# Graph attention on one core: in the score stages VectorE sums six heads instead of four, and ScalarE builds the one-hot matrices

## The reference

```
q = (x @ Wq[l] + bq[l]).reshape(N, H, D)      # N 2500 nodes, H 8 heads, D 64
k = (x @ Wk[l] + bk[l]).reshape(N, H, D)
v = (x @ Wv[l] + bv[l]).reshape(N, H, D)
a = (q[dst] * k[src]).sum(-1) * scale         # one score for each edge and head
e = jnp.exp(a - amax[dst])
alpha = e / (denom[dst] + 1e-16)
agg = jax.ops.segment_sum(alpha[:, :, None] * v[src], dst, num_segments=N)
x = agg.reshape(N, C) + (x @ Ws[l] + bs[l]) + enc
```

## Time and profile before

| what | us |
|---|---|
| median of 3 runs | 2849.92 |
| the profiled execution | 2865.84 |
| its span, first to last instruction | 2864.0 |
| score stage of layer 0, first to last multiply | 114.3 to 709.6 |
| score stage of layer 1, first to last multiply | 1378.5 to 1972.3 |

### The profile page before, as it was taken

The page is one execution under the profiler, slowest core; times in us unless marked ns, Lnnn a source line. Parts: engine busy times, 40 slices in busy tenths (PEclk is TensorE's granted clock), DMA queues, the critical chain, the costliest instruction groups (busy, mean ns, idle before and its releaser), DMA issues. The chain is left out here.

```text
span 2864.0 us, 41493 instructions
## 1 busy us (share of the span) xinstructions
PE 2088.5 (73%) x7660; PEld 1573.9 (55%) x7661; DVE 1771.3 (62%) x2574; ACT 1526.7 (53%) x8378; POOL 1509.9 (53%) x1499
## 2 busy tenths in 40 slices
PE   8677778775366877778677777773566666677997
PEld 6455555553355656666455555542455555565786
DVE  7465666667655555556466666667554555567895
ACT  3266666666455455555466666664454554453221
POOL 1355555554665555551655555554555565544663
PEclk9888888887688888889798888886788888888999
DMA  8666767664666666653776767675555555543111
GB/s 300 224 205 206 220 199 221 210 205 149 202 178 187 192 191 190 191 181 117 238 212 211 216 201 215 203 214 159 159 154 154 156 167 155 156 123 129 52 67 43
DMA packets 201657, 511.74 MB, mean 179 GB/s; under 512 B 37916, under 2 KB 60572, under 8 KB 201191
## 3 DMA queue, kind: packets, MB, share of 16 engines
q0 software_dynamic: 112832, 369.71, 44.3%
q1 hardware_dynamic: 85862, 135.89, 14.2%
q10 hardware_dynamic: 2880, 5.24, 0.6%
HBM read 451.33 MB, written 59.06 MB: 178 GB/s over the span
## 5 line engine op out<-in xcount | busy, mean ns | idle before, releaser
L1255 PE MATMUL coll_banks<-coll_ev,coll_hot 128*128 128x260 f32 x2816 | 778.0, 435 | 301.0 <-DVE all_work L1359 257.9
L652 POOL DMA_INDIRECT all_work<-k_rows,all_work x704 | 673.7, 957 | 517.7 <-DVE all_work L881 280.0
L652 POOL DMA_INDIRECT coll_rows<-v_rows,coll_index x704 | 670.3, 952 | 502.6 <-issue 207.0
L1255 PEld LDWEIGHTS coll_banks<-coll_ev,coll_hot 128*128 128x128 f32 x2816 | 601.0, 218 | 457.4 <-DVE all_work L1359 258.3
L984 ACT ACTIVATE all_work<-all_work 128x64 f32<-128x64 f32 x2752 | 665.9, 243 | 233.0 <-issue 188.5
L846 PE MATMUL score_q_ps<-score_q,score_hot 128*128 x1408 | 474.2, 466 | 295.5 <-DVE score_hot L872 108.9
L881 DVE TENSOR_TENSOR all_work<-score_q_ps,all_work 128x1024 f32<-128x1024 f32 x352 | 430.2, 1222 | 381.5 <-remote 161.4
L984 ACT ACTIVATION_READ_ACCUMULATOR all_work<-all_work 128x1 f32 x2752 | 519.9, 189 | 160.3 <-issue 159.6
L1359 DVE TENSOR_TENSOR all_work<-all_work,coll_banks 128x520 f32 x352 | 244.3, 694 | 499.0 <-DMA score_w_raw<-in_Ws 177.2
L1515 ACT ACTIVATE coll_ev<-coll_rows,coll_e_now 128x64 f32<-128x64 f32 x2112 | 537.2, 333 | 0.0
L846 PEld LDWEIGHTS score_q_ps<-score_q,score_hot 128*128 128x128 f32 x1408 | 302.3, 225 | 422.8 <-issue 364.8
(11 more groups left out here) (251 smaller groups left out, 2342.2 us busy)
## 6 DMA issues: line engine op xcount, KB each, us to landing
score_xt<-x_turned SPq DMA_DIRECT2D x42, 512.0 KB
all_work<-k_rows,all_work POOLq DMA_INDIRECT x704
score_local<-local_dst SPq DMA_DIRECT2D x176, 64.0 KB
coll_rows<-v_rows,coll_index POOLq DMA_INDIRECT x704
x_turned<-keys_xt SPq DMA_DIRECT2D x20, 512.0 KB
score_skip<-in_x SPq DMA_DIRECT2D x40, 256.0 KB
v_rows<-score_v_out SPq DMA_DIRECT2D x40, 256.0 KB
skip_rows<-score_skip SPq DMA_DIRECT2D x40, 256.0 KB
```

Source lines behind the costliest of these rows:

```text
L652: nc.gpsimd.indirect_dma_start(rows[:, slot, t, :], None, table, at).then_inc(arrived[slot], 16)
L1255: last = nc.tensor.matmul(sums[s % SUMS][:, part, :], m, ev[:, s % EVS, t, part * AGG // 2:(part + 1) * AGG // 2], start=t == 0, stop=t == ...
```

## The change

DVE sums six heads of each tile (128 x 768) in all steps, the last 16 too, and ACT the other two, with 4 activations a step. `one_hot` moves from DVE to ACT. It now has two activations: Square of (partition number minus local number), with its own semaphore `squared`, and Relu of one minus that, which is 1 where the difference is 0 and 0 elsewhere. ACT issues the pair ahead of the sums of each even step, behind the same wait for the multiply.

```diff
-DVE_HEADS1, DVE_HEADS2 = 4, 5
-LAST_HEADS1 = 5
+DVE_HEADS1, DVE_HEADS2 = 6, 5
...
-                def one_hot(part, slot, times):
-                    dve.wait_ge(local_in[part], 16 * times)
-                    nc.vector.tensor_scalar(hot[:, slot, :], local[:, part, :], k.iota_col[:, 0:1], None,
-                                            ALU.is_equal).then_inc(hot_ready, 1)
...
-                            if s % HOT_STEPS == 0 and not (ends and s == HALF - HOT_STEPS):
-                                ahead = s // HOT_STEPS + 1
-                                one_hot(ahead % LOCALS, ahead % 2, half + ahead // LOCALS + 1)
...
+                def one_hot(pair, part, slot, times):
+                    act.wait_ge(local_in[part], 16 * times)
+                    nc.scalar.activation(hot[:, slot, :], local[:, part, :], ACT.Square, bias=k.iota_col[:, 0:1], scale=-1.0
+                                         ).then_inc(squared, 1)
+                    act.wait_ge(squared, pair + 1)
+                    nc.scalar.activation(hot[:, slot, :], hot[:, slot, :].bitcast(F32), ACT.Relu, bias=k.ones[:, 0:1], scale=-1.0
+                                         ).then_inc(hot_ready, 1)
...
                         act.wait_ge(multiplied, n + RING + 1)
+                        if s % HOT_STEPS == 0 and not (ends and s == BODY - HOT_STEPS):
+                            ahead = s % HALF // HOT_STEPS + 1
+                            one_hot(PAIRS * half + ahead, ahead % LOCALS, ahead % 2, half + ahead // LOCALS + 1)
                         for t in range(TPS):
                             for h in range(heads, HEADS):
...
-                body(FULL + 1, ((True, False), (False, False)), LAST_HEADS1, True)
+                body(FULL + 1, ((True, False), (False, False)), DVE_HEADS1, True)
```

More of the change, by code:

```diff
@@ L693, in score @@
         local_in = [ph.sem(f"local_in{i}") for i in range(LOCALS)]
-        hot_ready, q_ready = ph.sem("hot_ready"), ph.sem("q_ready")
+        squared, hot_ready, q_ready = ph.sem("squared"), ph.sem("hot_ready"), ph.sem("q_ready")
         multiplied, act_summed, dve_summed = ph.sem("multiplied"), ph.sem("act_summed"), ph.sem("dve_summed")
@@ L936, in body @@
                         add_up(n + HALF - 1, HALF - 1, heads)
-                one_hot(0, 0, 1)
                 q_low(0)
@@ L969, in weight_high @@
                     nc.scalar.activation(split_at[i][0][:], w_raw[:, i], ACT.Copy).then_inc(w_hi, 1)
+                one_hot(0, 0, 0, 1)
                 q_hi(0)
@@ L973, in _, with body @@
                     weight_high(0)
-                def body(it, sides, heads, weights=False):
+                def body(it, sides, heads, weights=False, ends=False):
                     for s in range(BODY):
@@ L1002, in _ @@
                 body(FULL, ((True, True), (False, True)), DVE_HEADS1)
-                body(FULL + 1, ((False, False), (False, False)), LAST_HEADS1)
+                body(FULL + 1, ((False, False), (False, False)), DVE_HEADS1, False, True)
         ph.give_back()
```

## The result

The changed kernel takes 2819.59 us (median of 6 runs, 2804.97 to 2835.96) against 2850.27 for the kernel before (6 runs, 2846.3 to 2864.99) beside it: ratio 0.9878, 95% interval 0.9842 to 0.9913. That is 31 us gained where 202 were forecast, outside the range: a real gain, as the interval leaves out 1, but a small one. The profiled execution of the changed kernel is its fastest run, 2804.97 us (span 2803.2), and that of the kernel before lies 16 us above its median, so about half of the 61 us between the two profiled spans belongs to these two executions.

What follows compares the result with a forecast made beforehand. ACT, with its unexplained stalls, was taken to set the 3.40 us score step. DVE's 2.37 plus 0.48 from stretches less 0.03 gave 2.82 us, saving 202 us: 2648 us forecast, range 2560 to 2765.

Steps and rivals of the forecast that it cites:

- ACT, bad stretches: Score stages: ACT idles without cause once per 67 of its instructions, 4.0 us each, so 0.69 us a step instead of 1.05.
- So ACT sets the step: Score stages before the change: ACT busy 2.23 us and idle without cause 1.05 of each 3.40 us step.
- A bad stretch of 4.0 us therefore reaches DVE with about 4.0 - 1.2 = 2.8: Score stages: ACT's slack of 1.2 us absorbs part of each stretch, leaving DVE 0.48 us a step.
- DVE's stall-free pace: Score stages after the change: DVE takes 2.37 us a step when nothing stops it.
- POOL's floor: Score stages: POOL's two gathers a step need 2.51 us, under the forecast step of 2.82.
- ACT's one-hot: Score stages: each 512-element activation takes 0.63 us, a pair 1.36 us, or 0.68 a step.
- this sign of being wrong: Score stages: waits for one-hot matrices taking ACT's place with more than 100 us in 550 would show the forecast wrong.
- Hidden by 0.8: Multiply, ACT's one-hot pair, PE, next multiply but one: 3.9 us for two steps against DVE's 4.7, at full PE clock.
- A count explains the first two: Stretch spacings in the loop and the last 16 steps match 67 and 68 ACT instructions between stretches.
- Rival 2: Score stages: stretches come by time while gathers flow, each 12.8 us, giving 3.16 us a step and 2766 us; chance 0.16.
- Rival 1's end case: Score stages: stretches vanish when ACT asks less often, POOL binds at 2.51 us, 2553 us; chance of all rival 1 0.26.
- Rival 3: Score stages: low PE clock binds, 3.5 us a step, 35 us slower, 2885 us; chance 0.07.

Runs made afterwards that it cites:

- e7: Kernel before with DVE summing six heads and ACT two, one-hot compare still on DVE, slow chip: 2841.59 us against 2889.49, ratio 0.9823.
- e8: Changed kernel with only the first of each score step's two key-row gathers, slow chip: 2515.92 us against 2889.49, ratio 0.869.
- e20: Kernel before with direct transfers of 128 contiguous rows in place of the score stages' indirect gathers, fast chip: 2154.9 us, ratio 0.9702.
- e15: Changed kernel with direct transfers of 128 contiguous rows in place of the score stages' indirect gathers, fast chip: 2189.44 us, ratio 0.9871.
- e16: Changed kernel unaltered, on a fast chip: 2212.23 us against 2217.82 for the kernel before, ratio 0.9975.
- e5: Changed kernel unaltered, run again on a slow chip: 2828.58 us against 2850.07 for the kernel before, ratio 0.9914.
- e10: Changed kernel with as many gathers but rows of 1 KB instead of 2, slow chip: 2854.15 us, ratio 0.9872.

## Why the prediction was wrong, step by step

**The failed step is "ACT, bad stretches: ... At 67 between stretches they come each 5.8 steps", with "So ACT sets the step" before it and "A bad stretch of 4.0 us therefore reaches DVE with about 4.0 - 1.2 = 2.8" behind it.** That ACT's own sums stall, and that DVE waits for them, was read rightly, but it is 0.40 of 1.22 us that DVE stands idle a step in the table above, so ACT sets the step only in part. And the stretches are not ACT's. Two spacings were made into a count of its instructions, and what stalls is whatever runs or is awaited when a stretch comes: ACT's sums before, the releases of PE's and DVE's own work afterwards. ACT's instructions fell by 40%, and in e7 its busy time by half, and DVE still stood idle 0.9 to 1.1 us a step; with half of the gathers it was 0.12, at the same ACT work.

**In the sum** the term was 0.48 us a step and is 0.93, the measured 3.28 less DVE's stall-free 2.35. Part of the miss is in how often (one stretch in 3.9 and 3.3 steps in two traces, where 5.8 were forecast), part in how much (3.0 to 3.4 us of DVE's time each, where 2.8 were forecast). The rest is small, and of both signs.

- DVE's stall-free pace: forecast 2.37, measured 2.35 (e8, on kind B). The reduction took 0.943 as forecast.
- DVE's work: +0.07 forecast, +0.08 busy by e20 and e15, and the step +0.10.
- POOL's floor: forecast 2.51, measured 2.50 (e16).
- ACT's one-hot: 0.722 us, not 0.63, so a pair is about 1.5. The rows of 1024 and 2048 elements have 0.83 ns an element and 0.20 us fixed; this form, whose bias comes from SBUF, has 0.30 fixed. The Trainium skill ("ScalarE: Activation LUTs", What ACT_TABLE_LOAD costs) says that each such operand adds about 93 ns, and by its 280 ns + 0.833 ns an element an estimate for 512 elements is 706 ns; the trace agrees with 722. PE waited longer for one-hot matrices, 97 us in 530 against 48 in 550. That is 101 in 550, so this sign of being wrong came true by a hair, as did the other, a stage above 560 us. It cost DVE 0.17 us a step more (0.30 against 0.12 to 0.15 in the table). That most of it stands behind late multiplies is likely, since PE's wait is 32 us in 410 in e15.
- "Hidden by 0.8", of the hot chain, held without stretches: in e8 and e15 the step is DVE's.
- "A count explains the first two": two spacings fit a count of many things. With the stretches counted as in e7 above, they come each 53 instructions of ACT before and 36 in the changed kernel (its sequencer's own left out of both). Gathers don't give a fixed count either: 6.5 before, 7.8 changed, 9.1 in e7. The forecast noted that no stretch is seen once POOL has nothing left to ask for, and did not use it.
- "In the collect stage ACT runs 956 activations with no idle ahead of them": this took one group of rows for the stage. The group that starts each tile's weighting had the idle time, most of it put down to a DMA again:

```profile
L1510 ACT ACTIVATE coll_ev<-coll_e_now 128x16 f32<-128x16 f32 x160 | 33.8, 211 | 216.7 <-DMA x_turned<-keys_xt 152.8 <-PE coll_banks L1255 52.7 <-issue 10.9
```

That is 217 of 540 us, ahead of 160 instructions. On kind A (e16, 620 to 1000 us) it is 18 us ahead of 158. The collect stages, 540 to 576 us on kind B and 406 to 412 on kind A, have such stretches too (DVE stands 7.8 us in the longest), and they have no accumulator reads.

**The rivals.** Rival 2 ("by time while gathers flow", 2766 us) was nearest. It let stretches take 3.2 of 12.8 us, 25%; in the changed kernel stalls take 0.93 of 3.28, 28%, and stretches lie 12.8 us apart (10.9 in e5). Its 0.8 us of ACT's slack absorb nothing of what holds DVE directly. But a fixed period is not the rule either: in e7 stretches lie 15.3 us apart. Rival 1's end case, stretches vanish and POOL binds at 2.51, is what kind A shows. Rival 3 did not come: the clock is 0.87.

**Where the 31 us come from.** On kind B heads alone give as much (0.9823) as the whole change (0.9914 and 0.9878), with overlapping intervals and on another chip, so there the one-hot half adds nothing that these runs can tell. The table has the rest: DVE no longer waits for ACT (0.58 us a step with the wait ahead of `q_low`), late releases take 0.23 more, waiting for PE 0.17 more and DVE's own work 0.06 more, which leaves 0.12 us a step. That a stretch which no longer finds ACT at its sums shows as a late release fits this; no run isolates it.

**What stays open.** What a stretch is, and why some chips have them and others not. That they go when every second gather goes is shown (e8), and so is that halving the bytes alone leaves them (e10). Whether it is the indirect form, or its 0.95 us of issue without a gap, is not: the three runs that would tell met kind A. Whether a pause helps on kind B.

## What to carry to other kernels

Idle time whose releaser is "issue", "remote" or a DMA long finished, on more engines than one, need not be that engine's: before costing a change to it, list what every engine did at that moment, and look whether the idle time only moves to another engine. To say that a stage has no idle time, look at all groups of an engine, not at the busiest. Price moved work by the engine that is the limit once the stalls are gone: here the change took work off ACT and put 0.06 to 0.10 us a step on DVE. The same edit was worth 0.9 to 1.2% on one kind of chip and 0.25% on the other, so a forecast of time needs the chip's own trace.

## What the runs showed of the hardware

- One program takes 2218 us on some chips and 2850 to 2889 us on others. The stages with POOL's gathers make the difference; the 114 us ahead of them and the 286 behind are alike. On the slow kind, with two indirect gathers a step, DVE stands idle 0.9 to 1.2 us a step; with one, 0.12.
- In a stretch, ACT's sums, which wait for nobody, go one in 1.3 to 1.4 us instead of 0.24 (396 to 399 us of the kernel before).
- In the late stretch shown, the updates that did land between 420.1 and 424.5 us came some 0.70 us apart (at 420.19, 420.88, 421.59, 422.33, 422.99, 423.71 and 424.45, one to three together), and ten lie in 0.45 us from 424.45 on. All up to 423.71 are those of DMAs. Two instructions of SP's sequencer, a check and a move, took 0.70 us each in it, where the same took 0.02 and 0.03 us shortly before. I know of no cause.
- An indirect gather of 128 rows costs POOL 0.95 us, with rows of 1 KB as with rows of 2 KB, and 0.30 more before the next; a direct transfer of 128 rows 0.54 us.
- Behind a 0.14 us memset with a wait for it, POOL's next gather starts 0.88 us later.
